# Flamingo block on one core: the last two attention units put in another order, and the rows of maxima on their own semaphores

## The reference

```python
x = x + jnp.tanh(g_xattn[0]) * _L0_xattn_ref(_layernorm(x), ctx_1024, w_q, w_k, w_v, w_o)
x = x + jnp.tanh(g_ffn[0])   * _L0_ffn_ref(_layernorm(x), gate_w, gate_up_w, down_w)
# _L0_xattn_ref: 16 heads of 8
attn = jax.nn.softmax(jnp.einsum('bqhd,bkhd->bhqk', q, k) * scale, axis=-1)
out = jnp.einsum('bhqk,bkhd->bqhd', attn, v).reshape(B, T_q, D_MODEL) @ w_o.T
# _L0_ffn_ref: 8 experts of width 512, softmax router, the best 2 of 8, weights made to sum to 1
gu = jnp.einsum('th,efh->etf', x, gate_up_w); gate, up = gu[..., :F], gu[..., F:]
expert_out = jnp.einsum('etf,ehf->eth', up * gelu(gate), down_w)
out = jnp.einsum('eth,te->th', expert_out, combine)
```

## Time and profile before

| what | value |
|---|---|
| median of 3 runs | 285.87 us (285.84 to 286.03) |
| profiled execution, its own time | 286.03 us |
| its span, first to last instruction | 284.3 us |
| PE busy | 272.7 us (96%) |
| DVE busy | 215.2 us (76%) |
| ACT busy | 181.6 us (64%) |
| mean granted TensorE clock | 0.996 |
| chain that ended last, by engine | PE 85%, DVE 7%, ACT 4%, issue 2% |

### The profile page before, as it was taken

How to read it: one execution, slowest core, us unless ns; L and a number is a source line. 1 busy time by engine, 2 the same in 40 slices (tenths; PEclk the granted TensorE clock), 3 DMA queues, 4 the chain that set the end, 5 groups by cost and what they waited for, 6 DMA issues and landing times.

```text
span 284.3 us, 8055 instructions
## 1 busy us (share of the span) xinstructions
PE 272.7 (96%) x2823; PEld 221.9 (78%) x2823; DVE 215.2 (76%) x426; ACT 181.6 (64%) x370; POOL 97.9 (34%) x114
## 2 busy tenths in 40 slices
PE   7988999999999999999999998999979999999994
PEld 3465878878878878887887888887877879999962
DVE  4678797697967978779778797798447788888761
ACT  2736776687766777678667775466727877776500
POOL 3598832242053043133215201022610755554200
PEclk9999999999999999999999999999999999999998
DMA  7397945942980991794496199300000000000001
GB/s 254 106 205 197 222 111 166 242 143 82 233 231 1 260 243 40 177 238 128 124 242 177 41 217 268 136 0 2 2 2 0 1 0 2 0 1 0 0 0 32
DMA packets 9924, 32.19 MB, mean 113 GB/s; under 512 B 2576, under 2 KB 3088, under 8 KB 9904
## 3 DMA queue, kind: packets, MB, share of 16 engines
q1 hardware_dynamic: 9472, 31.60, 43.3%
q10 hardware_dynamic: 432, 0.33, 0.4%
HBM read 13.26 MB, written 0.23 MB: 47 GB/s over the span
## 4 chain that ended last, share of the span: by engine, by line
PE 85%; DVE 7%; ACT 4%; issue 2%; DMA 1%; SPq 0%; POOL 0%; DVEq 0%; ACTq 0%
PE max_ps L981 16%; PE score_ps L961 15%; PE o_ps L995 14%; PE misc_ps L949 8%; PE misc_ps L943 5%; PE score_ps L1199 3%; DVE part_max L705 3%; PE score_ps L1200 2%; PE score_ps L1201 2%; PE o_ps L1301 2%; PE misc_ps L1041 2%; PE o_ps L1199 2%; PE o_ps L1200 2%; PE o_ps L1201 2%; PE max_ps L1004 2%
## 5 line engine op out<-in xcount | busy, mean ns | idle before, releaser
L705 DVE TENSOR_REDUCE part_max<-max_ps 112x1 f32<-112x512 f32 (+1 forms) x192 | 117.4, 672 | 33.4 <-PE max_ps L981 31.6
L517 ACT ACTIVATE probs<-score_ps 128x448 f32<-128x448 f32 x192 | 92.1, 546 | 16.0 <-PE score_ps L961 15.9
L981 PE MATMUL max_ps<-kx,qx 96*112 96x512 f32 (+1 forms) x192 | 82.0, 432 | 2.2 <-DVE part_max L705 1.2
L961 PEld LDWEIGHTS score_ps<-qx,kx 104*128 104x128 f32 (+1 forms) x384 | 69.1, 188 | 10.6 <-issue 1.9
L961 PE MATMUL score_ps<-qx,kx 104*128 104x224 f32 (+1 forms) x384 | 73.7, 276 | 0.6 <-DVE qx L724 0.4
L995 PE MATMUL o_ps<-probs,v_sb 128*32 128x112 f32 (+1 forms) x1536 | 44.5, 261 | 0.6 <-ACT probs L517 0.6
L981 PEld LDWEIGHTS max_ps<-kx,qx 96*112 96x112 f32 x192 | 33.6, 176 | 9.0 <-issue 4.9
L995 PEld LDWEIGHTS o_ps<-probs,v_sb 128*32 128x32 f32 (+1 forms) x1536 | 36.4, 110 | 3.1 <-ACT probs L517 0.8
L366 POOL TENSOR_TENSOR k_low<-k_full,k_high 128x512 fp32r<-128x512 f32 (+1 forms) x21 | 26.2, 1251 | 30.8 <-ACT k_full L500 30.5
L401 POOL TENSOR_TENSOR o_norm<-o_sb,inv_den 128x112 f32 (+1 forms) x15 | 6.3, 422 | 75.8 <-DVE inv_den L731 75.8
L512 ACT ACTIVATE v_sb<-misc_ps 128x512 f32<-128x512 f32 x24 | 14.5, 602 | 27.4 <-PE misc_ps L949 27.4
(11 more groups left out here) (187 smaller groups left out, 371.9 us busy)
## 6 DMA issues: line engine op xcount, KB each, us to landing
kx<-k_high SPq DMA_DIRECT2D x60, 187.5 KB, 5.2
kx<-k_low SPq DMA_DIRECT2D x30, 187.5 KB, 5.0
ctx_sb<-in_ctxT SPq DMA_DIRECT2D x7, 750.0 KB, 5.5
gu_sb<-in_guT SPq DMA_DIRECT2D x8, 512.0 KB, 5.4
dn_sb<-in_dnT SPq DMA_DIRECT2D x8, 256.0 KB, 5.5
ctx_sb<-in_ctxT SPq DMA_DIRECT2D x2, 256.0 KB, 4.0
kx<-k_high SPq DMA_DIRECT2D x4, 123.5 KB, 2.3
kx<-k_high SPq DMA_DIRECT2D x4, 64.0 KB, 2.0
```

The lines of the kernel that those rows point to most:

```text
L517: nc.scalar.activation(probs[:, (KT * h + t) % 8, :], score_ps[:, t % 3, 0:SC // 2], ACT.Exp, scale=SCALE).then_inc(exp_done, 1)
L705: nc.vector.reduce_max(part_max[:, p, c:c + 1], max_ps[0:PC, bank, 0:size], AX.X).then_inc(max_taken, turns)
L961: last = nc.tensor.matmul(score_ps[0:m, t % 3, GC * g:GC * g + GC], kx[0:KR, 2 * par + h, g, 128 * t:128 * t + m], qx[0:KR, par, 2 * h + g ...
L981: nc.tensor.matmul(max_ps[0:PC, bank, 0:size], qx[0:MR, par, 2 * h + p // 2, PC * (p % 2):PC * (p % 2) + PC], kx[0:MR, slot, p // 2, start ...
```

## The change

Six things are changed.

1. In units 0 to 13, the scores of tile 5 and of tile 11 now stand ahead of the product of maxima beside them, and not behind it.
2. The rows of maxima leave the ring: their matmul counts on `rows_done`, their writing on `rows_made`, and they always use bank 1 of `max_ps`, in which they stood before as well. The ring begins at `RING0 = 15` in place of 18. The wait for the ones in `kx` stands once in a loop pass in place of in each unit.
3. Ahead of the loop, the matmul of unit 0's rows stands before the value projection and not behind it, and DVE writes the rows between its two reductions.
4. Unit 14: its value products run in two runs of six, its denominators and inverse of unit 13 two turns later.
5. Unit 15: its score tiles go through five banks (three of `score_ps`, two of `max_ps`), its value products run in runs of 4, 5 and 3 tiles with a wait for each tile's exponential, and the last scores stand ahead of the second run.
6. The tokens are turned ahead of the last two runs, into a `score_ps` bank, and ACT copies them ahead of the sums of unit 15; DVE splits them (L817) ahead of the inverse and inverts unit 14's denominators inside the layer norm.

```diff
-LAST_RUN = 4
-LAST_RUNS = KT // LAST_RUN
-DEN, NEXT_ROWS, LATER = 6, 13, 10
-PV_ALL = RUNS * (NU - 2) + 2 * LAST_RUNS
+DEN, LATER, ROWS_BANK = 6, 10, 1
+LAST_RUNS = [(0, 4), (4, 9), (9, KT)]
...
-RING0 = UM + AHEAD + 3
+RING0 = UM + AHEAD
...
+        last_banks = [score_ps[:, 0, :], score_ps[:, 1, :], score_ps[:, 2, :], max_ps[:, 1, :], max_ps[:, 2, :]]
+        early_xT_ps = score_ps[:, 2, :]
...
-            def exp_tile(i, par, h, t):
+            def exp_tile(i, par, h, t, banks=None):
+                bank = banks[t % len(banks)] if banks else score_ps[:, t % 3, :]
                 act.wait_ge(scores_done, KT * unit(i, par, h) + t + 1)
-                nc.scalar.activation(probs[:, (KT * h + t) % 8, :], score_ps[:, t % 3, 0:SC // 2],
+                nc.scalar.activation(probs[:, (KT * h + t) % 8, :], bank[:, 0:SC // 2],
                                      ACT.Exp, scale=SCALE).then_inc(exp_done, 1)
...
+            o_copy(3, 1, 0)
             for t in range(KT):
-                exp_tile(3, 1, 1, t)
-                if t == 2:
-                    o_copy(3, 1, 0, PV_ALL - LAST_RUNS)
+                exp_tile(3, 1, 1, t, last_banks)
+            act.wait_ge(xT_done, 2)
+            nc.scalar.activation(xnT[:, 0:OWN], early_xT_ps[:, 0:OWN], ACT.Copy).then_inc(xT_saved, 1)
+            nc.scalar.activation(x_high[:, 0:OWN], early_xT_ps[:, 0:OWN], ACT.Copy).then_inc(xT_saved, 1)
             o_copy(3, 1, 1, PV_ALL)
-            act.wait_ge(xT_done, 2)
-            nc.scalar.activation(xnT[:, 0:OWN], xT_ps[:, 0:OWN], ACT.Copy).then_inc(xT_saved, 1)
-            nc.scalar.activation(x_high[:, 0:OWN], xT_ps[:, 0:OWN], ACT.Copy).then_inc(xT_saved, 1)
...
             def last_but_one(u):
-                for n in range(LAST_RUN):
+                for n in range(DEN):
                     take_max(ring(u, n), n % 3, AHEAD + n)
-                invert(u - 1, 1, ring(u, LAST_RUN), LAST_RUN % 3)
-                for n in range(LAST_RUN + 1, TAIL):
+                invert(u - 1, 1, ring(u, DEN), DEN % 3)
+                for n in range(DEN + 1, TAIL):
                     take_max(ring(u, n), n % 3, AHEAD + n - 1)
                 negate_max(u + 1, ring(u, TAIL))
-                max_rows(ring(u, TAIL), TAIL % 3, 1, 1)
+                max_rows(u + 1, ROWS_BANK, 1, 1)
...
-            attended(2, 0, NR - 1)
+            attended(2, 0, NR - 1, lambda: invert(NU - 2, 0, ring(NU - 2, TAIL), 0))
             nc.vector.memset(zeros.bitcast(f32), 0.0).then_inc(zeros_ready, 1)
-            invert(NU - 2, 0, ring(NU - 2, TAIL + 1), (TAIL + 1) % 3)
-            invert(NU - 1, 1, ring(NU - 2, TAIL + 2), (TAIL + 2) % 3)
-            dve.wait_ge(max_taken, ring(NU - 2, TAIL + 2) + 1)
-            nc.vector.tensor_tensor(o_norm[:, NR - 1, 2:4, 1, :], o_sb[:, PC:2 * PC].rearrange("p (s c) -> p s c", s=2),
-                                    inv_den[:, PC:2 * PC].rearrange("p (s c) -> p s c", s=2), ALU.mult
-                                    ).then_inc(o_norm_ready, 1)
...
+            invert(NU - 1, 1, ring(NU - 2, TAIL + 1), 1)
+            dve.wait_ge(max_taken, ring(NU - 2, TAIL + 1) + 1)
...
-            def scores(i, par, h, t, rows=0):
-                if t == 0:
-                    pe.wait_ge(max_taken, rows)
-                    pe.wait_ge(kx_ones, 2 * par + h + 1)
-                pe.wait_ge(exp_done, KT * unit(i, par, h) + t + FIRST_EXP - 2)
+            def begin(i, par, h):
+                pe.wait_ge(rows_made, unit(i, par, h) + 1)
+                if par == 0 and h == 1:
+                    pe.wait_ge(kx_ones, 4)
+            def scores(i, par, h, t, banks=None):
                 m = 128 if t < KT - 1 else LAST
+                bank = banks[t % len(banks)] if banks else score_ps[:, t % 3, :]
+                if banks is None or t < 3:
+                    pe.wait_ge(exp_done, KT * unit(i, par, h) + t + FIRST_EXP - 2)
+                elif t >= len(banks):
+                    pe.wait_ge(exp_done, KT * unit(i, par, h) + t + FIRST_EXP - len(banks) + 1)
                 for g in range(2):
-                    last = nc.tensor.matmul(score_ps[0:m, t % 3, GC * g:GC * g + GC],
+                    last = nc.tensor.matmul(bank[0:m, GC * g:GC * g + GC],
...
+                for t in range(first, end):
+                    if runs:
+                        pe.wait_ge(exp_done, KT * u + t + 1 + FIRST_EXP)
...
+            transpose_max(0, UM + 2, 2)
             pe.wait_ge(v_saved, NCH)
             v_project(1, 0)
-            transpose_max(0, UM + 2, 2)
-            for n in range(2, AHEAD):
-                max_scores(0, 0, 1, n, UM + 1 + n, (1 + n) % 3, turns=3 if n == AHEAD - 1 else 1)
+            pe.wait_ge(rows_made, 1)
+            max_scores(0, 0, 1, 2, UM + 2, 2)
+            pe.wait_ge(kx_ones, 1)
             pe.wait_ge(k_saved, 4 * NCH)
...
-            def attention(i, par, h, rows, job=project):
+            def attention(i, par, h, job=project):
                 u = unit(i, par, h)
                 u1, u2 = ahead(i, par, h, 1), ahead(i, par, h, 2)
-                for t in range(RUN):
+                for t in range(RUN - 1):
                     max_scores(*u1, AHEAD + t, ring(u, t), t % 3)
-                    scores(i, par, h, t, rows)
+                    if t == 0:
+                        begin(i, par, h)
+                    scores(i, par, h, t)
+                scores(i, par, h, RUN - 1)
+                max_scores(*u1, AHEAD + RUN - 1, ring(u, RUN - 1), (RUN - 1) % 3)
                 job(i, par, h, 0)
                 denominators(u - 1, 1 - h, ring(u, DEN), DEN % 3)
                 attend(i, par, h, 0)
...
                 for n in range(RUN + AHEAD, UM):
                     max_scores(*u1, n, ring(u, n - 2), (n - 2) % 3)
                     scores(i, par, h, n - AHEAD)
-                for n in range(AHEAD):
+                for n in range(AHEAD - 1):
                     max_scores(*u2, n, ring(u, LATER + n), (LATER + n) % 3)
                     scores(i, par, h, KT - AHEAD + n)
+                scores(i, par, h, KT - 1)
+                max_scores(*u2, AHEAD - 1, ring(u, LATER + AHEAD - 1), (LATER + AHEAD - 1) % 3, turns=3)
                 job(i, par, h, 2)
-                transpose_max(u + 1, ring(u, NEXT_ROWS), NEXT_ROWS % 3, turns=2)
+                transpose_max(u + 1, ring(u, LATER + AHEAD), ROWS_BANK)
                 attend(i, par, h, 1)
...
-            def transpose_tokens(first, end, ready):
+            def transpose_tokens(first, end, ready, bank=xT_ps):
...
-            for t in range(LAST_RUN):
+            for t in range(RUN):
                 last_max(AHEAD + t, t)
                 last_scores(0, t, t + 1)
-            denominators(NU - 3, 1, ring(NU - 2, LAST_RUN), LAST_RUN % 3)
-            for t in range(4, 7):
+            denominators(NU - 3, 1, ring(NU - 2, RUN), RUN % 3)
+            for t in range(RUN, 8):
                 last_max(AHEAD + t, t + 1)
                 last_scores(0, t, t + 1)
-            attend(3, 1, 0, 0, LAST_RUN)
-            for t in range(7, 9):
-                last_max(AHEAD + t, t + 1)
-                last_scores(0, t, t + 1)
-            last_scores(0, 9, 11)
-            attend(3, 1, 0, 1, LAST_RUN)
-            transpose_max(NU - 1, ring(NU - 2, TAIL), TAIL % 3)
+            last_max(UM - 1, TAIL - 1)
+            attend(3, 1, 0, 0)
+            last_scores(0, 8, 11)
+            transpose_max(NU - 1, ring(NU - 2, TAIL), ROWS_BANK)
             last_scores(0, 11, KT)
-            last_scores(1, 0, 3)
-            attend(3, 1, 0, 2, LAST_RUN)
-            last_scores(1, 3, 6)
-            denominators(NU - 2, 0, ring(NU - 2, TAIL + 1), (TAIL + 1) % 3)
-            last_scores(1, 6, 7)
-            attend(3, 1, 1, 0, LAST_RUN)
-            last_scores(1, 7, 11)
-            attend(3, 1, 1, 1, LAST_RUN)
-            transpose_tokens(0, NR - 1, NR)
-            last_scores(1, 11, KT)
-            attend(3, 1, 1, 2, LAST_RUN)
-            denominators(NU - 1, 1, ring(NU - 2, TAIL + 2), (TAIL + 2) % 3)
+            attend(3, 1, 0, 1)
+            last_scores(1, 0, 5)
+            denominators(NU - 2, 0, ring(NU - 2, TAIL), 0)
+            last_scores(1, 5, 8)
+            attend(3, 1, 1, 0, LAST_RUNS)
+            last_scores(1, 8, KT)
+            pe.wait_ge(exp_done, KT * (NU - 1) + 8 + FIRST_EXP)
+            transpose_tokens(0, NR - 1, NR, early_xT_ps)
+            attend(3, 1, 1, 1, LAST_RUNS)
+            attend(3, 1, 1, 2, LAST_RUNS)
+            denominators(NU - 1, 1, ring(NU - 2, TAIL + 1), 1)
```

53 lines of the change are left out of this document (29 added, 24 removed).

## The result

The changed kernel takes 283.15 us (median of four, 282.96 to 284.24), the kernel before on the same chip 285.95 (median of four): a ratio of 0.9896, with a 95% interval of 0.9876 to 0.9916 (a ratio under 1 is faster; it is not exactly the quotient of the two medians, which is 0.9902). That is 2.8 us by the medians and 3.0 by the ratio, beside a forecast of 2.56 and a predicted time of 283.3. The profiled execution took 283.05 us, its span 281.3, at a clock of 1.00.

The account below looks back on a forecast made before the run. PE's instructions bound the loop, where only waits can be won; in the tail PE and ACT wait for each other. Head 0.65, loop 0.65 and tail 1.26 sum to 2.56 us: 286.03 to 283.47 (283.3 from the median); range 282.2 to 284.9.

Parts of the forecast that it names:

- Ahead of the loop: Before the loop: earlier rows and a freed ring start DVE's reductions sooner; 0.65 us gained, bounds 0 and 0.8.
- the 0.22 that was reckoned for tile 5: Unit 0's first half: tile 5's scores, now ahead of the last product, take another 0.22 us out of what follows.
- In the loop: Loop and units 12 and 13: 13 units by 0.05 give 0.65 us, bounds 0 and 2.1.
- The first half's wait: First half of each unit: PE's wait of 0.05 us for DVE's reductions is covered by tile 5's scores.
- So PE comes 0.11 earlier and waits 0.11 longer: Second half of each unit: the next scores wait for the rows, so the 0.11 us covered counts as nothing.
- Rival C: Loop: the second half's waits count too, 0.11 x 13 us more gained, 281.9 us; chance 0.07.
- Rival A: Loop and head give nothing because the rows set each unit's time; the tail gives 1.26, 284.6 us; chance 0.13.
- Unit 14: Unit 14: the second run of six waits at its head for tile 11's exponential and loads at 198.7 us.
- The price: Unit 15's scores queue behind unit 14's second run and start at 199.9, not 198.65: 1.2 us.
- Unit 15: Unit 15: five banks let ACT go at its own pace; sums copied at 206.9, not 208.14; 1.26 us gained.
- Rival B: Tail: gain lost to unit 15's late start and to waits; head and loop give 1.3, 284.6 us; chance 0.13.
- rival D: Units 14 and 15: the clock falls in PE's pause before the second run; at most 7 us more, 290; chance 0.04.

Follow-up runs that it names:

- the repeats: Profiles of other runs that leave the 13 units as they are in the changed kernel; eight of them take 150.46 to 150.55 us there.
- the second experiment: Product of maxima ahead of tile 11's scores again in the second half of units 0 to 13, against the changed kernel; ratio 0.9885.

## Why the prediction was right

**Ahead of the loop: 0.65 forecast, 0.71 measured.** Each link came as written: the rows' matmul beside the first reduction, the rows behind it, DVE's six about 0.5 us sooner, the projection at 28.55 (28.6 forecast; on the count from the negation it is 28.40). Undoing the order alone gives back 0.48. The other 0.23 is about the 0.22 that was reckoned for tile 5, but the old order of the first six gives back only 0.07 of it in this stretch; where the rest sits was not tried.

**In the loop: 0.65 forecast, 1.07 measured (0.97 by the repeats); here a term was too small.** The first half's wait was sized rightly (0.05 a unit, 0.61 to 0.71 for 13). The step that failed is "So PE comes 0.11 earlier and waits 0.11 longer", which put the second half at nothing. The runs show 0.24 to 0.34 us there, and 0.12 more in the tail. The argument forgot what DVE does behind the rows: its next six start when PE has brought the next product. DVE's idle there falls from 0.29 to 0.21 with the change and is 0.34 with the second half's old order put back, so a part of the 0.11 is passed on to the next half. How 0.08 to 0.16 us of DVE's idle in a unit become only about 0.02 in the unit's length was not followed. Rival C (all 0.11 counts, 1.4 us more) fell: it needed at least three times as much. Rival A fell too.

**Unit 14: right to a tenth.** Counted from its first scores, the second run was forecast at 197.07 and came at 196.99, unit 15's first scores at 198.27 and 198.28, with the idle of 1.04 us that was named. The price, unit 15's first scores behind unit 14's rows, was reckoned at 1.2 us and is 1.26 (9.48 before, 10.74 now); the wait for each tile gave back 0.91 of it. Off this path the forecast missed: the negation came 0.4 and the rows 0.27 sooner than reckoned. DVE went from its first reduction of unit 14 to the negation in 6.10 us, and not in 6.44.

**Unit 15: 1.26 forecast (its own times, 208.14 and 206.9, make 1.24), 1.32 measured for both units.** On the same count its first exponential was forecast at 198.77 and came at 198.81, the tokens at 202.37 and 202.46, the copy of the sums at 205.27 and 205.19. The three banks showed that the gain hangs on ACT's freedom: all of it goes when two of the five are taken away. Smaller steps missed and cancelled: turning the tokens took 0.66 on the chain and not 0.85; the split of the tokens took DVE 0.99 us. Rival B (the gain lost to the late start) fell, by the old tail's 1.25.

**The clock.** The pause before unit 14's second run left the granted clock at 1.00, here and in every stretch of the tail, so rival D fell. The prediction read the Trainium skill (TensorE: Matmul & The Clock Gate, "HAM oscillation — how this bites in real kernels") as speaking for D. That section's own case is a matmul kernel that waits for a transfer at every step, longer than PE pauses here; it does not say that a pause of this length brings the clock down. This case's traces show a clock of 1.00 through pauses of 1.04 us and, in the kernel before, 1.46 us. The 0.76 at the very end of the kernel before was no measure of what such a pause does: the end of the changed kernel, with as much work, shows 1.00, and other executions 0.78 to 1.00.

```profile
277.00:281.30 4.30, 1.10 (x8) 0.90 (x8) 1.12 (x4) 0.00 (x0) 0.00 (x0) 1.00 0.18 53
```

## What to carry to other kernels

When two engines hand one another tiles through few banks, neither full, look for banks that are idle at that point of the program: here the whole gain of a tail hung on two borrowed banks, and the new order without them gave nothing. A wait for the last tile at the head of a run holds all that is queued behind it; waiting tile by tile was worth 0.9 us here. And before a piece is moved off one chain, look at what stands ahead of the next piece in the same queue: twice a gain of half a microsecond ended in front of the router's matmuls.

## What the runs showed that was not expected

- Kernels that are the same up to unit 0's maxima reached that place between 23.03 and 24.12 us of their spans. That is as much as the effects looked for, so a single end time could not have told them.
- One transfer of context took 8.5 us from issue to landing in one execution (the one of the second experiment), where the median of the seven of its kind was 5.8, and cost PE 0.8.
- ACT's exponentials of 448 columns follow each other at 0.44 us or so while one is shown 0.54 long (eight in 3.60 us with three banks): the pace is not the duration.
